# Slot lists found by counting, and each addition into the output split into two column halves

## What is computed

```python
logits = xf @ router_w.T                          # 4096 x 64
scores = softmax(logits)
topk_w, topk_idx = top_k(scores, 8)
topk_w = topk_w / (topk_w.sum(-1, keepdims=True) + 1e-20)
onehot = one_hot(topk_idx.reshape(-1), 64)
pos = (cumsum(onehot, axis=0) * onehot).sum(-1) - 1
valid = pos < 128                                 # CAP: first 128 tokens of each expert
dest = where(valid, slot_expert * 128 + pos, 64 * 128)
...
slot_out = yb[dest] * topk_w.reshape(-1)[:, None]
out = zeros((4096, 512)).at[slot_token].add(slot_out)
```

## Time and profile before

| | us |
|---|---|
| median of 3 runs | 3461.34 (3455.7 to 3472.47) |
| the profiled execution | 3456.27 |
| its span, first to last instruction | 3454.1 |
| PE busy | 3128.1 (91%) |
| PEld busy | 2440.1 (71%) |
| DVE busy | 1855.5 (54%) |
| ACT busy | 1257.1 (36%) |
| POOL busy | 1606.5 (47%) |

### The profile page before, as it was taken

How to read it: one execution, slowest core, us unless ns; L and a number is a source line. 1 busy time by engine, 2 the same in 40 slices (tenths; PEclk the granted TensorE clock), 3 DMA queues, 4 the chain that set the end, 5 groups by cost and what they waited for, 6 DMA issues and landing times. The chain is left out here.

```text
span 3454.1 us, 45609 instructions
## 1 busy us (share of the span) xinstructions
PE 3128.1 (91%) x16217; PEld 2440.1 (71%) x16217; DVE 1855.5 (54%) x3969; ACT 1257.1 (36%) x2827; POOL 1606.5 (47%) x1410
## 2 busy tenths in 40 slices
PE   5999999899999989999998999999858099999996
PEld 3777777777878777787877778787637067676764
DVE  5455556655555565555566555556528852434431
ACT  3344444334434333433333343343352023232322
POOL 2366657624554653455465244545511154444352
PEclk8999999999999999999999999999889599999998
DMA  6433223352223234211222421221073168787876
GB/s 211 157 114 105 97 89 104 131 170 99 89 86 108 89 106 156 86 62 68 80 87 91 154 73 62 80 92 50 22 251 119 36 181 225 205 213 205 220 206 141
DMA packets 219406, 424.95 MB, mean 123 GB/s; under 512 B 22448, under 2 KB 102960, under 8 KB 217136
## 3 DMA queue, kind: packets, MB, share of 16 engines
q1 hardware_dynamic: 200624, 377.99, 32.7%
q0 software_dynamic: 18560, 44.05, 6.8%
HBM read 311.22 MB, written 110.69 MB: 122 GB/s over the span
## 5 line engine op out<-in xcount | busy, mean ns | idle before, releaser
L776 POOL TENSOR_SCALAR probs<-probs,comb 128x512 f32<-128x512 f32 (+3 forms) x384 | 221.6, 586 | 1018.2 <-DVE comb L725 1018.0
L897 ACT ACTIVATE probs<-score_ps,neg_max 128x640 f32<-128x640 f32 (+7 forms) x512 | 374.4, 738 | 481.5 <-DVE neg_max L731 481.5
L731 DVE TENSOR_REDUCE neg_max<-score_ps 128x2 f32<-128x256 f32 (+7 forms) x256 | 347.2, 1356 | 114.4 <-PE score_ps L1025 113.4
L781 POOL TENSOR_TENSOR probs<-probs 128x512 f32<-128x512 f32 (+3 forms) x384 | 383.9, 1014 | 10.7
L785 POOL TENSOR_TENSOR out_root<-out_root,neg_half 128x16 f32<-128x16 f32 x128 | 372.5, 2911 | 4.8 <-DVE out_root L708 4.8
L820 ACT ACTIVATE attT<-turn_ps 128x512 fp32r<-128x512 f32 (+3 forms) x384 | 189.0, 492 | 470.6 <-PE turn_ps L934 468.3
L633 DVE TENSOR_TENSOR layer_sum<-product_ps,layer_sum 128x512 f32<-128x512 f32 x384 | 262.9, 685 | 30.8 <-PE product_ps L40 24.6
L1022 PE MATMUL score_ps<-keys_all,queries_all 64*128 64x512 f32 (+3 forms) x2304 | 278.0, 364 | 0.0
L620 DVE TENSOR_TENSOR attT<-turn_ps,attT 128x512 fp32r<-128x512 f32 (+3 forms) x384 | 212.7, 554 | 106.6 <-ACT attT L820 103.9
L678 DVE SCALAR_TENSOR_TENSOR hidden<-gate_tanh,product_ps 128x512 f32<-128x512 f32 x128 | 88.0, 688 | 312.7 <-ACT gate_tanh L862 312.7
L1022 PEld LDWEIGHTS score_ps<-keys_all,queries_all 64*128 64x128 f32 x2304 | 187.6, 186 | 67.4 <-issue 31.1
(11 more groups left out here) (253 smaller groups left out, 7293.9 us busy)
## 6 DMA issues: line engine op xcount, KB each, us to landing
w_qk<-weights_split SPq DMA_DIRECT2D x48, 512.0 KB, 4.6
w_gate<-weights_split SPq DMA_DIRECT2D x48, 512.0 KB, 3.3
w_up<-weights_split SPq DMA_DIRECT2D x48, 512.0 KB, 3.6
w_down<-weights_split SPq DMA_DIRECT2D x48, 512.0 KB, 6.8
e_gate_up<-in_w_gate_dram SPq DMA_DIRECT2D x64, 384.0 KB
e_gate_up<-in_w_up_dram SPq DMA_DIRECT2D x64, 384.0 KB
e_down<-in_w_down_dram SPq DMA_DIRECT2D x64, 384.0 KB
values_by_head<-hidden_split SPq DMA_DIRECT2D x32, 512.0 KB, 3.3
```

The source lines that it names most:

```text
L731: dve.tensor_reduce(nmax[:, i % 2, :], score_tile(i % NT), AX.X, ALU.max, negate=True)\
L776: pool.tensor_scalar(PR[:, r, 1, c], PR[:, r, 1, c], comb[:, i % 4:i % 4 + 1], 1.0, ALU.mult, ALU.mult)\
L781: pool.tensor_tensor(PR[:, r, 0, c], PR[:, r, 0, c], PR[:, r, 1, c], ALU.add).then_inc(s_comb, 1)
L897: act.activation(PR[:, i % 2, q, 0:(j + 1) * P], score_tile(j)[:, q, :], ACT.Exp, bias=nmax[:, i % 2, q:q + 1], accum_out=sums[:, i % 16, ...
```

## The change

It replaces the drawing by counting. `sel` becomes bf16 with the expert ahead of the tile of 128 tokens, and:

- ("cum", q), four items: TensorE multiplies the mask with a triangular matrix `upto`, which gives, for each expert and tile, the running count of chosen tokens within the tile; ScalarE copies the counts out as bf16.
- ("starts",): one product with `below` gives the count at each tile's start.
- ("window", 0 to 3): four VectorE operations over 2048 columns find which of the 128 slot numbers fall into which tile, and their number within it (`inside`, `past`).
- ("find", g), sixteen: for four experts each, TensorE lays running count minus slot number into a PSUM bank; ("near", g): VectorE marks where it is at most zero; ("counted", g): products with one column add the marks up, so that the slot's token number comes out as a count.
- ("slot",): five small operations on VectorE instead of four, which also give the row numbers of two halves of each output row (`halves`).

The maxima, replacements, the transposes of the mask, the move and the merge go. The column item of the last sequence comes one projection after the first instead of after the fourth, the planner may run scan operations before the slot lists are done, and expert 0 starts one step after the slot list instead of two. SP loads expert 0's gate and up weights at ("counted", 14), and expert 0's down and expert 1's gate and up weights at ("weights",) of expert 0's step, behind that step's `load_gate_up(2)` and `load_down(1)`.

Each addition into the output, 64 of experts and 8 of the recurrence, becomes two of 256 columns each, in two chains of waits (`s_chain[0]`, `s_chain[1]`); who waited for one link now waits for both.

Followed step by step, the planner's rules give this plan (items and VectorE's slot work; the rest follows the same pattern):

| step | before | step | after |
|---|---|---|---|
| 43 to 67 | the 24 projections of sequence 0, cols 3, keep 3; early 4 to 15, top, sel, key; draw 0 to 3 | 43 to 50 | 7 projections, cols 3, keep 3, top 3, sel 3, cum 0 to 3, starts |
| 68 to 75 | 8 turns | 51, 52 | 2 projections; window 0 to 3 |
| 76 to 87 | draw 4 to 15 | 53 to 62 | 10 projections; find 0 to 15, near, counted, scan operations |
| 88 to 95 | move, merge 0 to 15, slotturn, slot | 63 | 1 projection; slot |
| 97 | expert 0 | 64 | expert 0, weights, 2 projections |
| 157 to 160 | experts 60 (outp 3 6, outp 3 7, yadd 3 1) to 63 | 124 to 128 | experts 60 (outp 3 6, outp 3 7) to 63, then yadd 3 1 |

The core of the diff:

```diff
-                for r in range(6 * (b - 1), min(6 * b, ROUNDS)) if b else ():
-                    yield ("early", r), 2.6
             yield ("zsum",), 2.4
-            for r in range(ROUNDS):
-                yield ("draw", r), 3.0 if r + 1 < ROUNDS else 1.5
-                if r == 3:
-                    yield ("topsum",), 2.4
-                    yield ("den",), 0.8
-            for r in range(ROUNDS):
-                yield ("merge", r), 1.0
-            yield ("slot",), 1.5
+            for q in range(4):
+                yield ("window", q), 1.6
+            yield ("topsum",), 2.4
+            yield ("den",), 0.8
+            for g in range(NG):
+                yield ("near", g), 0.7
+            yield ("slot",), 0.6
...
+                                if (o, w, c, h) == (0, 0, 0, 0):
+                                    yield ("cols", batches - 1), 0.9
...
-                    if todo[0][0][0] == "due" and todo[0][0][1:] not in done and route:
+                    if todo[0][0][0] == "due" and route:
...
+                            if k == "sel" and b == batches - 1:
+                                later += [(s + 1, ("cum", 0)), (s + 1, ("cum", 1)), (s + 2, ("cum", 2)), (s + 2, ("cum", 3)),
+                                          (s + 3, ("starts",))]
+                                ready["start"] = s + 3
...
+                            if k == "window" and b == 3:
+                                for g in range(NG):
+                                    find_at[g] = s + 1 + g // 2
+                                    later.append((find_at[g], ("find", g)))
...
-                                started = s + 2
-                    if scans and scans[0][0:2] in gates_at and not took and (started is not None or not route):
+                                started = s + 1
+                                later.append((s + 1, ("weights",)))
+                    if scans and scans[0][0:2] in gates_at and not took:
...
+                        if v == ("counted", NG - 2):
                             sp.wait_ge(s_gst, 16)
                             sp.wait_ge(s_pad, 32)
-                            sp.wait_ge(s_left, 2 * ROUNDS - 1)
+                            sp.wait_ge(s_found, NG - 2)
                             load_gate_up(0)
+                        if v[0] == "weights":
+                            sp.wait_ge(s_slot, 3)
+                            load_down(0)
                             load_gate_up(1)
-                            load_down(0)
...
+                    if kind == "window":
+                        if b == 0:
+                            dve.wait_ge(s_start, 1)
+                            dve.tensor_tensor(past[:, :, :], slot_no.unsqueeze(1).to_broadcast([P, NG, P]),
+                                              start.unsqueeze(2).to_broadcast([P, NG, P]), ALU.subtract).then_inc(s_win, 1)
+                        if b == 1:
+                            dve.wait_ge(s_win, 1)
+                            dve.tensor_tensor(inside[:, :, :], past[:, :, :], count[:, :, P - 1:P].to_broadcast([P, NG, P]),
+                                              ALU.is_lt).then_inc(s_win, 1)
+                        if b == 2:
+                            dve.wait_ge(s_win, 2)
+                            dve.scalar_tensor_tensor(inside[:, :, :], past[:, :, :], 0.0, inside[:, :, :], ALU.is_ge, ALU.mult)\
+                               .then_inc(s_win, 1)
+                        if b == 3:
+                            dve.wait_ge(s_win, 3)
+                            dve.tensor_tensor(past[:, :, :], past[:, :, :], inside[:, :, :], ALU.mult).then_inc(s_win, 1)
+                    if kind == "near":
+                        dve.wait_ge(s_find, b + 1)
+                        if b >= 2:
+                            dve.wait_ge(s_found, b - 1)
+                        dve.tensor_scalar(near[:, b % 2, :], free[b % BANKS][:, :], 0.0, None, ALU.is_le).then_inc(s_near, 1)
...
+                        for h in range(2):
+                            dve.tensor_scalar(halves[:, h, :], tmp[:, :], pad[:, h:h + 1], 2.0, ALU.add, ALU.mult).then_inc(s_slot, 1)
...
-                    if link["expert", n]:
-                        pool.wait_ge(s_chain, 16 * link["expert", n])
-                    pool.indirect_dma_start(out, bass.IndirectOffsetOnAxis(slots[:, n:n + 1], 0), ys[:, n % 3, :], None,
-                                            compute_op=ALU.add).then_inc(s_chain, 16)
+                    for h in range(2):
+                        if link["expert", n]:
+                            pool.wait_ge(s_chain[h], 16 * link["expert", n])
+                        pool.indirect_dma_start(out.rearrange("t (h n) -> (t h) n", h=2),
+                                                bass.IndirectOffsetOnAxis(halves[:, h, n:n + 1], 0),
+                                                ys[:, n % 3, h * (D // 2):(h + 1) * (D // 2)], None,
+                                                compute_op=ALU.add).then_inc(s_chain[h], 16)
...
-                            if link[v]:
-                                pool.wait_ge(s_chain, 16 * link[v])
-                            pool.dma_start(tile_rows(out, TURNS[o], 4 * q, 4).rearrange("(t p) n -> p t n", p=P), Y[:, q],
-                                           accum_op=ALU.add).then_inc(s_chain, 16)
+                            for h in range(2):
+                                part = slice(h * (D // 2), (h + 1) * (D // 2))
+                                if link[v]:
+                                    pool.wait_ge(s_chain[h], 16 * link[v])
+                                pool.dma_start(tile_rows(out, TURNS[o], 4 * q, 4)[:, part].rearrange("(t p) n -> p t n", p=P),
+                                               Y[:, q, :, part], accum_op=ALU.add).then_inc(s_chain[h], 16)
...
+                    if v[0] == "cum":
+                        q = v[1]
+                        act.wait_ge(s_cum, q + 1)
+                        act.activation(count[:, G * q:G * q + G, :].rearrange("p g n -> p (g n)"), free[q % BANKS][:, :], ACT.Copy)\
+                           .then_inc(s_count, 1)
...
-                        act.wait_ge(s_chain, 16 * (link["expert", n - 3] + 1))
+                        act.wait_ge(s_chain[0], 16 * (link["expert", n - 3] + 1))
+                        act.wait_ge(s_chain[1], 16 * (link["expert", n - 3] + 1))
...
+                    if v[0] == "cum":
+                        q = v[1]
+                        pe.wait_ge(s_sel, batches)
+                        if q == 0:
+                            pe.wait_ge(s_whole, 7)
+                            pe.wait_ge(s_rows, 2 * batches)
+                            pe.wait_ge(s_lg, batches)
+                        if q >= BANKS:
+                            pe.wait_ge(s_count, q - BANKS + 1)
+                        for j in range(G):
+                            g = G * q + j
+                            ins = pe.matmul(free[q % BANKS][:, j * P:(j + 1) * P], sel[:, G * g:G * g + G, :].rearrange("p e i -> p (e i)"),
+                                            upto, start=True, stop=True)
+                        ins.then_inc(s_cum, 1)
+                    if v[0] == "starts":
+                        pe.wait_ge(s_count, NG // G)
+                        pe.matmul(start, below, count[:, :, P - 1], start=True, stop=True).then_inc(s_start, 1)
+                    if v[0] == "find":
+                        g = v[1]
+                        pe.wait_ge(s_win, 4)
+                        if g >= BANKS:
+                            pe.wait_ge(s_near, g - BANKS + 1)
+                        j, rows = g % G, slice(g % G * NTT, (g % G + 1) * NTT)
+                        for i in range(G):
+                            at, dst = g // G * G + i, free[g % BANKS][:, i * P:(i + 1) * P]
+                            pe.matmul(dst, count[rows, at, :], inside[rows, at, :], start=True, stop=False)
+                            ins = pe.matmul(dst, minus[rows, :], past[rows, at, :], start=False, stop=True)
+                        ins.then_inc(s_find, 1)
+                    if v[0] == "counted":
+                        g = v[1]
+                        pe.wait_ge(s_near, g + 1)
+                        if g == 0:
+                            pe.matmul(found, minus[:, :], none[:, :], start=True, stop=False)
+                            for at in range(NG):
+                                pe.matmul(found[:, 2 * G * at:2 * G * (at + 1)], inside[:, at, :], tile_one, start=False, stop=False)
+                        for i in range(G):
+                            e = G * (g // G * G + i) + g % G
+                            ins = pe.matmul(found[:, 2 * e:2 * e + 2], near[:, g % 2, i * P:(i + 1) * P], one_none, start=False,
+                                            stop=(g == NG - 1 and i == G - 1))
+                        ins.then_inc(s_found, 1)
```

192 lines of the change are left out of this document (79 added, 113 removed).

## The result

The changed kernel took 3438.6 us (median; 3434.4 to 3441.7) against 3459.7 for the kernel before beside it: a ratio of 0.9933, 95% interval 0.9909 to 0.9957. That is 21 us less where some 75 were forecast, and outside the range. The profiled execution has a span of 3435.9 us, 53.3 more than the 3382.6 of the sum.

A forecast was written before the change was run, and what follows sets the result against it. TensorE was taken to bound the kernel, with idle places of 93.6 us (slot list) and 32.6 us (additions). TensorE's end at 3350.9 plus 31.7 gave a span of 3382.6; plus 2.2, 3385 us, range 3357 to 3420.

The forecast's parts named there:

- The gap: TensorE's idle stretch before expert 0, waiting for the slot list, goes entirely: -93.6 us, with small costs in its place.
- 226 matmuls: New small bf16 matmuls of the counting on TensorE, taken at 0.08 us each: +18 us (13 to 26).
- Find 0's wait: Before the first find, TensorE waits for VectorE's four windows, put at 4.6 to 9.1 us: +2 us (0 to 8).
- The additions: Output additions after TensorE's end: expert period 5.1 us, recurrence link 13.3; program ends 31.7 us after TensorE, against 32.6 before.
- half price: Output additions: a half row costs half of a whole one, landing at 3.9 us with a period of 4.6 us.
- B: Rival, output additions: half rows cost as much as whole ones, doubling 181 us of DMA; about 3440 us, chance 0.09.
- A: Rival, finds: TensorE waits at each of 8 pairs for VectorE's reading of the banks; 3415 us, chance 0.12.
- C: Rival, output additions: their chain becomes the bound, halves running one after the other; slower, up to 3526 us, chance 0.03.
- D: Rival: no shorter addition link, and the gap before expert 0 shrinks by under a quarter; 3450 us, chance 0.03.
- the order after the change: Plan: expert 0 in step 64; 4 projections (10.9 us) and 8 turns (9.8 us) move among the experts, TensorE's work unchanged.
- The clock: TensorE from expert 0 on: without the long idle time it should stay at 2.4 GHz: -3 us.
- The +3 us for DMA waits: Expert stage: GpSimd issues twice the additions, half-size packets at half price change nothing, some waits remain: +3 us.

The follow-up runs named there:

- one chain: Changed kernel, counting kept, with every addition into the output whole again in a single chain of waits: 3440.5 us, ratio 0.9951.
- the two planner rules: Changed kernel; recurrences start at least one step after their last projection and gates, no tile turned in the step of the tile four before: 3393.1 us.

## Why the prediction was off

The 53.3 us by which the span is over the sum are 4.6 at the start of the stage, 59.6 in the stage and -10.9 behind it.

**The gap: right.** TensorE's idle 93.6 us went as the sum says, with the plan's steps as followed (find in 53, slot in 63, expert 0 in 64), and expert 0's transposes started at 2674.6 instead of 2670 us. Its small terms, one by one:

- 226 matmuls, +18 (13 to 26): from find 0 (2626.0) to the last projection's end (2672.2) are 46.2 us, of which 11 projections of 2.73 are 30.0; so 16.2 us for 209 small matmuls with their short waits and the lower clock behind find 0's wait, 0.078 each. Right.
- Find 0's wait, +2 (0 to 8): 5.01 us. The bound held, the value was low. The four windows took 7.27, 2.29, 2.29 and 1.23 us, 13.1 in all, over their upper bound of 9.1: I had them from a reduction alone, and put nothing on GpSimd's product beside them.
- Expert 0's start, +2: 3.0 (2.35 on the gathered rows and 0.68 on ScalarE). Weights of expert 1, +4: 3.91. Both right.
- Before 2594.5 us, -2: the first projection starts at 2594.23, not 2594.77, -0.5. This decides nothing: in the other traces with the change it starts between 2592.3 and 2597.7.

**The additions: mainly the size of one term.** Behind the last transposes, where TensorE is through but for the last down product (3413.2 us), the program takes 22.7 us; the forecast had 33.6 (31.7, and the 1.9 by which its E lies past them). The period of two experts' links was 4.68 us (5.1; 4.6 to 5.7), a half landed in 3.92 as under "half price", but the recurrence's link took 7.3 where I kept 13.3, the whole addition's:

```profile
3414.20 2.75 POOL L1856 DMA_DIRECT2D out_dram<-rec_out  x2 [1.36 <-DMA out_dram<-e_y,slot_halves]
3421.54 1.64 POOL L1798 DMA_INDIRECT out_dram<-e_y,slot_halves  x1 [4.60 <-issue]
3426.22 1.55 POOL L1798 DMA_INDIRECT out_dram<-e_y,slot_halves  x1 [1.15 <-DMA out_dram<-e_y,slot_halves]
```

I had taken less for a half of an expert's addition and kept the whole price for the recurrence's: 6.0 of the 10.9 us. It also started 1.0 us behind the transposes and not 4.4. With one chain, but this plan, that addition landed in 8.71 us, so the halving alone is not what took off most.

**Rivals.** B (half rows as dear as whole) is refuted by the queues, 2680 to 3400 us:

```profile
q1 hardware_dynamic: 30848, 95.17, 40.5%
q0 software_dynamic: 29190, 40.53, 31.6%
```

That is 0.316 x 720 x 16 = 3640 engine-us for the software queue, no more than the 3775 of before in a window of about the same length, where B adds 2900; by 29190 it is 0.125 a packet, where it was 0.203. The stage's DMA share fell to 0.73. A did not come, the steps of the finds kept TensorE's pace after find 0. C and D did not come either. (The 664 us in which the prediction sets GpSimd's issues and B's 699 us follow from none of its rows; its own sum gives the stage 680.9.)

**The expert stage: the step that failed.** It is the sentence on the order after the change, "TensorE's work is the same, only its order differs". I priced the moved work at its busy time, the weights' wait, 3 us of DMA waits and a better clock, and took the rest as it was: 680.9 us, or 679.0 by the marks used here. It took 738.6. Of the 59.6 us more, 34.4 are idle time (58.5 against 17.1 + 4 + 3) and 25.2 are work at a lower clock (680.1 against 637.2 + 20.7 - 3). The idle part is mainly 13.6 us for the gates of the second recurrence, 9.1 for three projections in second place, 5.2 more on the loads of rows, and 4.5 more on the copies behind the recurrence. The plan that I had followed for the steps' numbers showed the pairings behind the largest of them: gates (0, 1) and the first scan operation both in step 67, and the pairs of projections. I read from it when things start, not who stands beside whom. My first repair in mind, to let the hidden product pass, was wrong too (3439.5 us); the two planner rules show the cause, and with them the time is 3393.1 us, within the forecast's own 3360 to 3408. That it comes within 8 us of the forecast is in part luck: the stage is still 11.6 us longer than forecast, and the end is 11.5 us shorter.

**The clock** was forecast at 2.4 GHz throughout, since the long gap goes. It went down not once for 94 us but at every wait of some us, and cost about as much again as the waits: 22.5 us of busy time between the changed kernel and the one with the rules, beside 25.5 of idle time. The Trainium skill (TensorE: Matmul & The Clock Gate, HAM oscillation) tells of this form of loss, short waits that throttle TensorE again and again; these traces agree (0.53 to 0.84 behind the waits shown, 1.00 from 2820 to 2940 us).

**Halves as waits.** The +3 us for DMA waits was right in sign: TensorE waited 1.3 and 2.4 us longer than before for two loads of rows (4.19 and 4.07 against 2.85 and 1.67). But with one chain they are 3.48 and 2.71, so of these 3.7 us at most 2.1 are the halves'.

## What to carry to other kernels

In a kernel whose engines walk through one plan, a change that moves the start of a stage moves every cut behind it: list for each step which operation waits for an item of the same step, before and after, since that pairing can cost most of what the removed gap gives (59.6 of some 75 us here, with the lower clock behind the waits). When a queue stalls on an operation whose input is late, moving one victim ahead helps nothing (15.5 us reappeared a few instructions on); give the input a step of its own. Test such a cause by shifting the cuts of the unchanged kernel: one number there cost 49 us.

## What the runs showed of the hardware

VectorE operations with two operands in SBUF stood still while a GpSimd operation over 2048 columns ran. In the changed kernel:

```profile
2615.11 7.27 DVE L1682 TENSOR_TENSOR slot_in_tile<-without_top,running_count 128x2048 bf16<-128x2048 bf16 x1
2614.60 5.64 POOL L1829 TENSOR_TENSOR route_exp<-route_exp,selected 128x2048 f32<-128x2048 f32 x1
2629.77 0.68 DVE L1695 TENSOR_SCALAR tokens_ahead<-gu_ps 128x512 bf16<-128x512 f32 x1
2630.97 3.45 DVE L1619 TENSOR_TENSOR scan_diff<-scan_diff,forget 128x1024 f32<-128x1024 f32 x1
2628.86 4.47 POOL L1832 TENSOR_TENSOR route_exp<-route_exp,top_sum 128x2048 f32<-128x2048 f32 x1 [8.62 <-DVE top_sum L1674]
```

The window lay 5.13 us beside GpSimd's product and ran 2.14 us past its end, and took 2.29 us where nothing lay beside it; the scan operation took 3.45 instead of 1.22, while the one that reads from PSUM beside the same GpSimd operation kept its 0.68. The Trainium skill (SBUF — State Buffer, SBUF: two separate sides) says that the two engines share one pair of ports, which the first to start holds for its whole instruction; the trace agrees for these operations. It does not for a small one: beside GpSimd's power over 8 columns (L1848, 1.75 us at 2992.76 and 2.04 at 3189.37) a scan operation over 1024 columns, begun later, kept its 1.22 us (2993.49 and 3190.40). Beside the issue of a DMA it kept them too (2798.66).

Matmuls over 32 partitions, two finds in neighbouring row groups (the second writes y_ps), ran into each other: the second's first began before the first's last.

```profile
2626.44 0.28 PE L2064 MATMUL y_ps<-slot_in_tile,running_count 32*128 32x128 bf16 x1
2626.75 0.31 PE L2065 MATMUL gu_ps<-without_top,minus_one 32*128 32x128 bf16 x1
```

At the full clock the next such pair took 0.79 us for its 16 matmuls (2631.55 to 2632.34), 0.049 each; within one find they started 0.056 apart. So this overlap saved some 0.1 us of 0.9, far from the half that the prediction gave as the most.

An addition of 512 rows of the recurrence took 6.08 us to land as a half in the chain that ended last, where the whole one took 12.86; with one chain and the plan of the changed kernel it took 8.71, as the same chain there has it:

```profile
3406.61 8.71 DMA out_dram<-rec_out
```

So most of the shorter link at the end is not the half's: about 4 us of it are there with one chain too, where the addition stands later in the plan, and 2.6 come with the half. No run tells the place in the plan from what else runs beside it.
